# Another order for the prologue and for the bridge between the two halves of a fused Mamba-2 and ternary-expert layer

## The chip, the cores and the metric

The kernel runs on one core of one Trainium2 chip. The metric is the device time of one execution in microseconds (us), the median of several. Five engines have their own instruction streams: TensorE (PE; its weight loads are shown apart as PEld), VectorE (DVE), ScalarE (ACT), GpSimd (POOL) and SyncE (SP, which here only issues DMAs). They meet through semaphores.

## The reference, cut to what matters

```python
def reference(u, ...):                      # u: (2, 2048, 512) float32
    zxbcdt = einsum('bld,ed->ble', u, W_in)          # 2184 outputs: z, x, B, C, dt
    dt  = softplus(zxbcdt[..., -8:] + dt_bias)
    xBC = silu(conv1d_depthwise_4_taps(xBC) + conv_b)
    y   = ssd(x, dt, -exp(A_log), B, C, D)           # chunked state-space scan, 8 heads of 128
    yg  = y * silu(z)
    yn  = yg * rsqrt(mean(yg*yg) + 1e-5) * norm_w
    x1  = layernorm(u + yn @ W_out.T)
    # expert: ternary weights, scale = mean|W|, q = clip(round(W/scale), -1, 1) * scale
    h   = silu(x1 @ up_q.T) * (x1 @ gate_q.T)        # 2048 hidden
    return layernorm(x1 + h @ down_q.T)
```

## The kernel before, in words

Everything is float32, multiplied as pairs of reduced-precision parts: a tensor is split into a high part (suffix `hi` or `h`, made by a copy on ACT) and the rest (`lo` or `l`, a subtraction on DVE or POOL), and three products (or two, with the exact ternary weights) stand for one.

**First half.** The 4096 tokens are done in 16 groups (n = 0 to 15) of 256 tokens, each of two chunks (c = 2n, 2n+1) of 128 tokens. For each group PE runs nine steps `ip(n, k)` of the input projection: k = 0 is feature tile 16 (B and C), k = 1 to 4 are tiles 8 to 15 (x), k = 5 to 8 are tiles 0 to 7 (z). They go round three PSUM banks, so that step r = 9n + k waits until what step r - 3 left has been read, by the convolution taps (`f_taps`, on DVE) or by the gate's activation (`f_zs`, on ACT). Between them stand the small products: `DT`, `dtT` and `CUM` for the time steps, `G` for C times B, the transposes `TR`, and per chunk `Y` (the output of the scan), `ST` (its state), `SQ` (the mean square) and `OP` (the output projection). On the other engines, `f_xe` empties a bank into the convolution, `f_silc` is the SiLU behind it (it needs `f_edge` on POOL, which carries the edge between groups), `f_seg`, `f_E` and `f_M` build the decay matrix, `f_DI` (POOL) finishes it, `f_xTe` empties the transposes, `f_gate` multiplies Y by the gate, `f_r1` and `f_x1` are the first layer norm.

**Prologue.** Groups 0 and 1 run while the weights are still being split. `split_in(j)` splits tile j of W_in: first the high part on ACT, in `WHI_ORDER`, then the low part on DVE (tiles of `DVE_LO`) or on POOL (tiles of `POOL_LO`). PE waits on a count of these, so a tile is free only when all tiles ahead of it in its list are done. `split_out(k)` does the same for W_out, by `WOHI_ORDER` (ACT) and `WOLO_ORDER` (DVE). All this is written out call by call, one list for each engine. Groups 2 to 15 then follow in a loop, each with the same body.

**The bridge.** Behind group 15 (c = 30 and 31 are its chunks) PE finishes the last chunks, transposes the first 512 tokens of x1 (`T1`, from `load_x1(0)`) and starts the expert for them (token group g = 0): 16 tiles j, each with `expert(j, 0)` (up), `expert(j, 1)` (gate) and `down(j)`. Its weights are made ternary on the fly: `load_tern(j)` on SP, `ternary(j)` on DVE (three comparisons at L1038, three selections at L1042). `f_sil`, `f_h`, `f_hh`, `f_hl` make and split the hidden values, and `down(j)` waits for `f_hl(j)`. Into the last third of this stretch the preparation of the next 512 tokens is laid: the transposes `TX(1, i)`, and `f_xa`, `f_xb`, `f_xd`, `f_xh`, `f_xl`, `f_th`, `f_tl`. Their halves are used from `pair_a(0)` on.

**Second half.** Token groups 1 to 7 run as 56 steps Q, each a pair of expert tiles in a form with seven products instead of eight (`pair_a`, `pair_b`, `pair_b3`, `pair_c`, L421), with `down` (L494) between them. The sums of weights that it needs are made by POOL the first time (`f_S123`, `f_S4`, L1336 to L1345), stored, and read back afterwards.

All orders are fixed in the program text. An engine that waits holds up everything behind the waiting call in its own list.

## Time and profile before

| | |
|---|---|
| device time, three runs | 1492.88, 1498.31 (the median), 1498.94 us |
| the profiled execution's own time | 1492.88 us |
| its span, first to last instruction | 1491.1 us |
| PE busy | 1467.0 us (98% of the span) |
| DVE, ACT, POOL busy | 1109.8, 885.6, 428.9 us |
| granted TensorE clock, mean | 0.998 of full speed |
| DMA | 151.36 MB, 102 GB/s over the span |

The busy shares are for the whole span. The prologue is the stretch up to about 84 us, where the loop over the groups begins. The bridge begins at about 760 us and ends at 876.5 us, where `pair_a(0)` starts. PE's matmuls overlap, so a matmul of 0.4 us starts some 0.23 us behind the one before it.

### The profile page before, as it was taken

To read this page: it belongs to the slowest core of one execution; us is meant where nothing else is said; L and a number is where in the kernel's file an instruction comes from. 1 tells how busy PE (TensorE), PEld (TensorE's weight loads), DVE (VectorE), ACT (ScalarE), POOL (GpSimd) and SP (SyncE) were. 2 spreads that over 40 slices of the span, in tenths; PEclk is the share of its full clock that TensorE was granted. 3 is DMA by queue.
4 is the path that set the end of the run, shared out by engine and by line. 5 is a ranking of instruction groups with operands and counts; after the bars stand their busy time and mean duration, and the time that the engine had idled before them with its cause. 6 is when DMAs were issued, how large, how long until landed. Compare 5 with 4: busy or idle time off the path is not lost.

```text
span 1491.1 us, 27358 instructions
## 1 busy us (share of the span) xinstructions
PE 1467.0 (98%) x10356; PEld 1315.5 (88%) x10356; DVE 1109.8 (74%) x2376; ACT 885.6 (59%) x1688; POOL 428.9 (29%) x536
## 2 busy tenths in 40 slices
PE   8999999999999999999989999999999999999997
PEld 8888898888888898889877789899999998999996
DVE  7877887788877887789779967766656666665655
ACT  8777767766677767766762244545454454545442
POOL 4344454444434454445451116300000000000000
PEclk9999999999999999999999999999999999999999
DMA  7111222022211222122244404343343434334341
GB/s 263 65 49 66 93 72 93 27 88 85 80 50 65 93 72 77 38 93 72 79 163 167 151 29 152 104 156 100 107 149 106 149 107 149 102 112 142 98 135 64
DMA packets 64050, 151.36 MB, mean 102 GB/s; under 512 B 6960, under 2 KB 7472, under 8 KB 63920
## 3 DMA queue, kind: packets, MB, share of 16 engines
q1 hardware_dynamic: 63920, 149.62, 30.1%
q8 instruction: 82, 1.34, 0.4%
q14 instruction: 48, 0.39, 0.1%
HBM read 124.30 MB, written 25.30 MB: 100 GB/s over the span
## 4 chain that ended last, share of the span: by engine, by line
PE 88%; DMA 5%; DVE 4%; ACT 1%; issue 1%; SPq 0%; POOL 0%; POOLq 0%; DVEq 0%; ACTq 0%
PE ps L258 25%; PE ps L421 23%; PE ps L494 13%; PE ps L347 11%; PE ps L301 3%; PE ps L411 3%; DMA s_S<-wsum_scratch 2%; PE ps L309 2%; PE ps L318 2%; PE ps L288 2%; DMA out_dram<-s_x1n 1%; PE ps L388 1%; DVE s_ltm L1038 1%; PE ps L274 1%; PE ps L231 1%
## 5 line engine op out<-in xcount | busy, mean ns | idle before, releaser
L258 PE MATMUL ps<-s_uhi,s_whi 128*128 128x256 f32 x1088 | 313.6, 288 | 3.6 <-POOL s_wlo L1254 1.8
L258 PE MATMUL ps<-s_uhi,s_wlo 128*128 128x256 f32 x1088 | 306.2, 281 | 0.0
L258 PE MATMUL ps<-s_ulo,s_whi 128*128 128x256 f32 x1088 | 306.2, 281 | 0.0
L421 PE MATMUL ps<-s_xoh,s_S 128*128 128x256 f32 x896 | 222.9, 285 | 2.8 <-DMA s_S<-wsum_scratch 2.5
L421 PE MATMUL ps<-s_xol,s_S 128*128 128x256 f32 x896 | 220.5, 282 | 0.0
L258 PEld LDWEIGHTS ps<-s_uhi,s_whi 128*128 128x128 f32 x1088 | 204.9, 188 | 9.0 <-issue 5.9
L258 PEld LDWEIGHTS ps<-s_ulo,s_whi 128*128 128x128 f32 x1088 | 205.1, 189 | 0.0
L258 PEld LDWEIGHTS ps<-s_uhi,s_wlo 128*128 128x128 f32 x1088 | 204.8, 188 | 0.0
L494 PE MATMUL ps<-s_tern,s_hh 128*128 128x512 f32 x504 | 199.3, 395 | 0.0
L494 PE MATMUL ps<-s_tern,s_hl 128*128 128x512 f32 x504 | 198.7, 394 | 0.0
L421 PEld LDWEIGHTS ps<-s_xoh,s_S 128*128 128x128 f32 x896 | 169.2, 189 | 12.8 <-DMA s_S<-wsum_scratch 4.9
L421 PEld LDWEIGHTS ps<-s_xol,s_S 128*128 128x128 f32 x896 | 169.6, 189 | 3.9
L1321 POOL TENSOR_TENSOR s_lnb<-s_lnb,s_cst 128x1 f32<-128x1 f32 x32 | 19.0, 597 | 515.4 <-DVE s_lnb L1169 515.4
L421 PE MATMUL ps<-s_xol,s_tern 128*128 128x256 f32 x672 | 164.2, 281 | 0.0
L421 PE MATMUL ps<-s_xoh,s_tern 128*128 128x256 f32 x672 | 164.2, 281 | 0.0
L869 DVE SCALAR_TENSOR_TENSOR s_xact<-ps,s_pm,s_xact 128x256 f32<-128x256 f32 x384 | 154.4, 473 | 0.8 <-ACT s_xact L587 0.7
L421 PEld LDWEIGHTS ps<-s_xoh,s_tern 128*128 128x128 f32 x672 | 126.5, 188 | 2.4
L421 PEld LDWEIGHTS ps<-s_xol,s_tern 128*128 128x128 f32 x672 | 126.4, 188 | 2.5
L948 DVE SCALAR_TENSOR_TENSOR s_mm<-s_mm,s_dtv,s_gm 128x128 f32<-128x128 f32 x256 | 116.7, 527 | 9.3 <-ACT s_mm L634 9.3
L1283 POOL TENSOR_TENSOR s_mm<-s_mm,s_di 128x1024 f32<-128x1024 f32 x32 | 77.4, 2418 | 141.1 <-DVE s_mm L948 141.1
L494 PEld LDWEIGHTS ps<-s_tern,s_hh 128*128 128x128 f32 x504 | 95.0, 188 | 14.9
L494 PEld LDWEIGHTS ps<-s_tern,s_hl 128*128 128x128 f32 x504 | 95.4, 189 | 14.4
(182 smaller groups left out, 3105.6 us busy)
## 6 DMA issues: line engine op xcount, KB each, us to landing
s_S<-wsum_scratch SPq DMA_DIRECT2D x48, 512.0 KB, 3.7
s_S<-wsum_scratch SPq DMA_DIRECT2D x96, 256.0 KB, 3.3
s_bcx<-ct_scratch SPq DMA_DIRECT2D x32, 512.0 KB, 4.8
s_wst<-in_wffn SPq DMA_DIRECT2D x48, 256.0 KB, 2.8
s_wraw<-in_wffn SPq DMA_DIRECT2D x16, 768.0 KB, 10.3
s_uraw<-in_uT SPq DMA_DIRECT2D x16, 512.0 KB, 3.7
s_rr<-in_un SPq DMA_DIRECT2D x32, 256.0 KB, 4.6
x_scratch<-s_rr SPq DMA_DIRECT2D x32, 256.0 KB, 2.4
```

The costliest lines, as they stand in the source:

```text
L258: o = e.matmul(IPB[r % 3][:, 256 * i:256 * i + 256], wt[:, j, kk, :], u[:, kk, :], start=(m == 0), stop=(m == 11))
L288: o = e.transpose(B0[half][:, 128 * i:128 * i + 128], xact[:, 4 * half + i, 128 * (c % 2):128 * (c % 2) + 128], ident)
L301: o = e.matmul(B0[a][:, 128 * i:128 * i + 128], xT[:, c % 3, 4 * a + i, :], mm[:, c % 2, 4 * a + i, :], start=(i == 0), stop=fresh(c) and ...
L309: o = e.matmul(B0[a][:, 128 * i:128 * i + 128], st[r, i, :], cx[r, c % 2, i, :], start=False, stop=(i == 3), skip_group_check=True)
L318: o = e.matmul(B3[64 * a:64 * a + 64, :], btr[:, c % 4, :], xw[:, c % 2, 4 * a:4 * a + 4, :].rearrange("p h s -> p (h s)"), start=True, st ...
L347: o = e.matmul(B2[:], y[:, h, :], wt[:, h, :], start=(m == 0), stop=(m == 23))
L411: o = e.matmul(bank[:], tern[:, j, 512 * mi + 128 * k:512 * mi + 128 * k + 128], x[:, k, :], start=(m == 0), stop=(m == 7))
L421: o = e.matmul(bank[:, 256 * mi:256 * mi + 256], wt(mi, k), xo[g % 2][:, x, k, :], start=(first and mi == 0 and k == 0 and xo is xoh), sto ...
L494: o = e.matmul(DB[c][:], y[:, 128 * c:128 * c + 128], tern[:, j, 1024:1536], start=(j == 0 and lo == 0), stop=(j == 15 and lo == 1))
L869: o = e.scalar_tensor_tensor(dst, bank[:, 256 * i:256 * i + 256], convw[:, f, 3 - shift:4 - shift], dst, mult, add)
L948: o = e.scalar_tensor_tensor(mm[:, m2, h, :], mm[:, m2, h, :], dtv[:, n % 2, 8 * odd + h:8 * odd + h + 1], gm[:, c % 4, :], mult, mult)
L1283: e.tensor_tensor(mm[:, c % 2, :, :], mm[:, c % 2, :, :], di[:], add).then_inc(s_DI, 1)
```

## The change

Nothing is added or removed. The same calls, with the same bodies, are put into another order, in two places: the prologue up to the loop, and the bridge up to `pair_a(0)`. The loop bodies of groups 2 to 15 and of the 56 pair steps are as before. Among other things:

- the split of the W_in tiles is dealt out anew: DVE now does the low parts of 16, 8, 9, 10 and 11, POOL the other twelve, in another order; the high parts come in another order too
- on PE, `dtT(0)` goes behind `ip(0, 1)`, `CUM(0)` behind `ip(0, 3)`, `TR(0, 0)` behind `dtT(1)`, `G(1)` ahead of `Y(0)`, and `ip(1, 4)` between `Y(0)` and `ST(0)`
- on ACT, `f_seg(1)` now stands ahead of `f_uhi(1)`, `f_zs(0, 3)` and `f_E(1)` stand ahead of `f_xe(1, 0)`, and `f_silc(1, 0)` ahead of `f_xTe(1, 1)`
- on SP, `load_r0` for chunks 0 and 1 comes later (chunk 1 behind `store_ct(2)`), and in the bridge `load_x1(1)`, which waits for `OP(31)`, comes behind `load_tern(7)` instead of behind `load_tern(4)`
- in the bridge, `Y(30)` goes ahead of `ST(30)`, `T1(0)` between; `f_E(31)` and `f_M(31)` are earlier; the calls of `down` come at other places, and `down(10)` and `down(11)` now stand ahead of `expert(13, 0)`

```diff
@@ -179,11 +179,11 @@
...
-    DVE_LO = [9, 8, 11, 12, 5]
-    WHI_ORDER = [16, 8, 9, 10, 12, 13, 11, 15, 0, 6, 2, 3, 14, 7, 1, 4, 5]
-    POOL_LO = [16, 10, 13, 14, 15, 1, 0, 6, 2, 3, 4, 7]
-    WOHI_ORDER = [0, 2, 4, 6, 1, 3, 5, 7]
-    WOLO_ORDER = [2, 0, 4, 3, 6, 7, 1, 5]
+    DVE_LO = [16, 8, 9, 10, 11]
+    WHI_ORDER = [16, 8, 9, 10, 12, 11, 13, 14, 15, 1, 0, 2, 3, 4, 7, 6, 5]
+    POOL_LO = [12, 13, 14, 0, 15, 1, 2, 3, 7, 6, 5, 4]
+    WOHI_ORDER = [2, 0, 4, 6, 3, 1, 5, 7]
+    WOLO_ORDER = [0, 4, 3, 2, 1, 6, 5, 7]
@@ -507,9 +507,9 @@
...
-        warm(); ip(0, 0); DT(0); dtT(0); ip(0, 1); ip(0, 2); CUM(0); ip(0, 3); ip(0, 4); G(0); ip(0, 5); ip(0, 6)
-        TR(0, 0); DT(1); ip(0, 7); ip(0, 8); dtT(1); TR(0, 1); ip(1, 0); ip(1, 1); TR(1, 1); TR(1, 0); CUM(1)
-        ip(1, 2); ip(1, 3); ip(1, 4); Y(0); ST(0); G(1); ip(1, 5); Y(1); OP(0); SQ(0); ip(1, 6); ip(1, 7); ip(1, 8)
+        warm(); ip(0, 0); DT(0); ip(0, 1); dtT(0); ip(0, 2); ip(0, 3); CUM(0); ip(0, 4); G(0); ip(0, 5); ip(0, 6)
+        DT(1); ip(0, 7); ip(0, 8); dtT(1); TR(0, 0); TR(0, 1); ip(1, 0); ip(1, 1); TR(1, 1); CUM(1); TR(1, 0)
+        ip(1, 2); ip(1, 3); G(1); Y(0); ip(1, 4); ST(0); ip(1, 5); Y(1); OP(0); SQ(0); ip(1, 6); ip(1, 7); ip(1, 8)
@@ -518,13 +518,13 @@
...
         c = NCH - 2
-        OP(c - 1); T1(1); WT(); ST(c); Y(c); T1(0); Y(c + 1); SQ(c); T1(2); T1(3); OP(c); expert(0, 0); expert(0, 1)
+        OP(c - 1); T1(1); Y(c); T1(0); WT(); ST(c); Y(c + 1); T1(2); SQ(c); T1(3); OP(c); expert(0, 0); expert(0, 1)
...
-        expert(4, 0); expert(4, 1); down(0); down(1); expert(5, 0); down(2); expert(5, 1); expert(6, 0); expert(6, 1)
-        down(3); expert(7, 0); down(4); expert(7, 1); expert(8, 0); expert(8, 1); expert(9, 0); expert(9, 1); down(5)
-        TX(1, 0); expert(10, 0); down(6); expert(10, 1); expert(11, 0); expert(11, 1); down(7); expert(12, 0); down(8)
-        TX(1, 1); expert(12, 1); expert(13, 0); down(9); expert(13, 1); expert(14, 0); down(10); expert(14, 1)
-        expert(15, 0); expert(15, 1); down(11)
+        expert(4, 0); expert(4, 1); down(0); expert(5, 0); down(1); expert(5, 1); down(2); expert(6, 0); expert(6, 1)
+        down(3); expert(7, 0); expert(7, 1); expert(8, 0); down(4); expert(8, 1); expert(9, 0); expert(9, 1); TX(1, 0)
+        expert(10, 0); down(5); down(6); down(7); expert(10, 1); expert(11, 0); expert(11, 1); down(8); expert(12, 0)
+        TX(1, 1); down(9); expert(12, 1); down(10); down(11); expert(13, 0); expert(13, 1); expert(14, 0)
+        expert(14, 1); expert(15, 0); expert(15, 1)
@@ -767,16 +767,16 @@
...
-        f_uhi(0); split_in(16); split_in(8); split_in(9); expA(); split_in(10); f_xe(0, 0); split_in(12); split_in(13)
-        split_in(11); split_in(15); split_in(0); f_spexp(0); f_silc(0, 0); f_xe(0, 1); split_in(6); split_in(2)
-        split_in(3); split_in(14); split_in(7); f_xe(0, 2); split_in(1); split_in(4); f_silc(0, 1); f_xe(0, 3)
-        wabs(0); f_silc(0, 2); f_xe(0, 4); split_out(0); split_in(5); f_silc(0, 3); f_seg(0); split_out(2)
-        f_silc(0, 4); f_seg(1); f_zs(0, 0); f_zs(0, 1); split_out(4); f_E(0); f_uhi(1); f_spexp(1); f_xTe(0, 0)
-        f_zs(0, 2); f_xTe(0, 1); split_out(6); f_zs(0, 3); wabs(1); f_xe(1, 0); f_dec(0); f_xe(1, 1); f_xTe(1, 0)
-        split_out(1); f_E(1); split_out(3); split_out(5); f_xe(1, 2); f_xe(1, 3); f_dec(1); f_xTe(1, 1); f_silc(1, 0)
-        f_silc(1, 1); split_out(7); f_xe(1, 4); f_silc(1, 2); f_sq(0); f_ygh(0); wabs(2); wabs(3); f_seg(2)
-        f_silc(1, 3); f_zs(1, 0); f_sq(1); f_zs(1, 1); f_ygh(1); f_zs(1, 2); f_silc(1, 4); f_seg(3); f_xTe(2, 0)
-        f_xTe(2, 1)
+
+        f_uhi(0); split_in(16); split_in(8); expA(); f_xe(0, 0); split_in(9); split_in(10); split_in(12); split_in(11)
+        split_in(13); split_in(14); f_xe(0, 1); split_in(15); f_spexp(0); split_in(1); split_in(0); f_silc(0, 0)
+        split_in(2); split_in(3); f_xe(0, 2); split_in(4); split_in(7); f_xe(0, 3); f_silc(0, 1); f_silc(0, 2)
+        wabs(0); f_xe(0, 4); split_in(6); f_silc(0, 3); split_in(5); split_out(2); f_silc(0, 4); split_out(0)
+        f_seg(0); split_out(4); f_zs(0, 0); f_zs(0, 1); f_E(0); f_seg(1); f_uhi(1); split_out(6); f_spexp(1); wabs(1)
+        f_xTe(0, 0); f_zs(0, 2); f_zs(0, 3); split_out(3); f_xTe(0, 1); f_E(1); f_dec(0); f_xe(1, 0); f_xTe(1, 0)
+        split_out(1); f_xe(1, 1); split_out(5); f_xe(1, 2); f_silc(1, 0); f_xTe(1, 1); f_xe(1, 3); f_dec(1)
+        f_silc(1, 1); split_out(7); f_sq(0); f_ygh(0); f_xe(1, 4); wabs(2); f_silc(1, 2); wabs(3); f_seg(2); f_ygh(1)
+        f_sq(1); f_zs(1, 0); f_silc(1, 3); f_zs(1, 1); f_zs(1, 2); f_silc(1, 4); f_seg(3); f_xTe(2, 0); f_xTe(2, 1)
...
             c = 2 * n - 2
@@ -796,11 +796,11 @@
...
         c = NCH - 2
-        f_xTe(c + 1, 1); f_zs(NG - 1, 3); f_E(c + 1); f_xTe(c + 1, 0); f_x1h(0); f_x1h(1); f_ygh(c); f_sq(c); f_x1h(3)
-        f_x1h(2); f_sil(0); f_sil(1); f_ygh(c + 1); f_sq(c + 1); f_sil(2); f_hh(0); f_hh(1); f_hh(2); f_sil(3)
-        f_sil(4); f_hh(3); f_sil(5); f_hh(4); f_sil(6); f_hh(5); f_sil(7); f_sil(8); f_hh(6); f_hh(7); f_hh(8)
-        f_sil(9); f_sil(10); f_xa(1, 0); f_hh(9); f_xh(1, 0); f_sil(11); f_hh(10); f_sil(12); f_xa(1, 1); f_sil(13)
-        f_hh(11); f_hh(12); f_th(1, 0); f_sil(14); f_xh(1, 1); f_hh(13); f_th(1, 1); f_hh(14); f_sil(15); f_hh(15)
+        f_E(c + 1); f_xTe(c + 1, 1); f_xTe(c + 1, 0); f_zs(NG - 1, 3); f_x1h(0); f_sq(c); f_ygh(c); f_x1h(1); f_x1h(3)
+        f_x1h(2); f_ygh(c + 1); f_sil(0); f_sq(c + 1); f_sil(1); f_hh(0); f_sil(2); f_hh(1); f_sil(3); f_sil(4)
+        f_hh(2); f_hh(3); f_sil(5); f_hh(4); f_sil(6); f_hh(5); f_sil(7); f_hh(6); f_sil(8); f_hh(7); f_sil(9)
+        f_hh(8); f_xa(1, 0); f_sil(10); f_hh(9); f_hh(10); f_xh(1, 0); f_sil(11); f_sil(12); f_xa(1, 1); f_hh(11)
+        f_th(1, 0); f_xh(1, 1); f_th(1, 1); f_sil(13); f_hh(12); f_sil(14); f_hh(13); f_hh(14); f_sil(15); f_hh(15)
@@ -1172,13 +1172,13 @@
...
-        f_ulo(0); split_in(9); split_in(8); setup(); f_dte(0); f_taps(0, 0); f_dtr(0); split_in(11); split_in(12)
-        f_dA(0); f_taps(0, 1); f_cte(0); f_taps(0, 2); f_taps(0, 3); f_GM(0); f_dd(0); f_taps(0, 4); split_in(5)
-        skip_diag(); f_dte(1); split_out(2); f_dd(1); split_out(0); split_out(4); f_dtr(1); f_ulo(1); f_dA(1); f_M(0)
-        f_taps(1, 0); f_cte(1); f_wz(0); f_taps(1, 1); f_M(1); split_out(3); f_taps(1, 2); f_gate(0, 0); f_GM(1)
-        f_gate(0, 1); f_S(0); split_out(6); split_out(7); split_out(1); split_out(5); f_sqsum(0); f_taps(1, 3)
-        f_taps(1, 4); f_gate(1, 0); f_gate(1, 1); f_ms(0); f_wz(1); f_dd(2); f_r1(0); f_sqsum(1); f_x1(0); f_S(1)
-        f_dd(3)
+        f_ulo(0); split_in(16); split_in(8); setup(); f_dte(0); split_in(9); f_taps(0, 0); split_in(10); f_dtr(0)
+        split_in(11); f_dA(0); f_taps(0, 1); f_cte(0); f_taps(0, 2); f_taps(0, 3); f_taps(0, 4); f_GM(0); skip_diag()
+        f_dte(1); split_out(0); split_out(4); f_dd(0); f_dd(1); f_dtr(1); f_ulo(1); f_dA(1); f_M(0); split_out(3)
+        f_cte(1); f_taps(1, 0); f_taps(1, 1); f_wz(0); f_M(1); f_taps(1, 2); f_gate(0, 0); split_out(2); f_S(0)
+        split_out(1); f_gate(0, 1); split_out(6); split_out(5); f_GM(1); split_out(7); f_sqsum(0); f_taps(1, 3)
+        f_taps(1, 4); f_gate(1, 0); f_wz(1); f_ms(0); f_gate(1, 1); f_sqsum(1); f_r1(0); f_dd(2); f_dd(3); f_S(1)
+        f_x1(0)
...
             c = 2 * n - 2
@@ -1193,14 +1193,14 @@
...
         c = NCH - 2
-        f_ms(c - 1); f_r1(c - 1); f_M(c + 1); f_gate(c, 0); f_gate(c, 1); f_x1l(1); f_S(c); f_sqsum(c); scales()
-        f_ms(c); f_x1l(0); f_x1l(2); ternary(0); f_x1l(3); ternary(1); f_gate(c + 1, 0); f_gate(c + 1, 1); f_h(0)
-        ternary(2); f_sqsum(c + 1); f_r1(c); ternary(3); f_h(1); ternary(4); f_x1(c - 1); f_hl(0); f_ms(c + 1)
-        f_hl(1); f_h(2); f_r1(c + 1); f_hl(2); f_h(3); ternary(5); f_h(4); ternary(6); f_hl(3); ternary(7); f_h(5)
-        f_hl(4); f_x1(c); f_hl(5); ternary(8); f_h(6); ternary(9); f_h(7); f_hl(6); f_h(8); ternary(10); f_x1(c + 1)
-        f_hl(7); f_hl(8); f_xb(1, 0); f_h(9); ternary(11); f_h(10); f_hl(9); ternary(12); f_xd(1, 0); f_h(11)
-        f_hl(10); ternary(13); f_xb(1, 1); ternary(14); f_h(12); f_xd(1, 1); ternary(15); f_hl(11); f_hl(12); f_h(13)
-        f_xl(1, 0); f_xl(1, 1); f_tl(1, 0); f_tl(1, 1); f_h(14); f_hl(13); f_hl(14); f_h(15); f_hl(15)
+        f_ms(c - 1); f_M(c + 1); f_r1(c - 1); f_gate(c, 0); f_gate(c, 1); scales(); f_S(c); f_x1l(1); f_sqsum(c)
+        f_x1l(0); f_ms(c); ternary(0); f_x1l(2); f_x1l(3); ternary(1); f_gate(c + 1, 0); f_gate(c + 1, 1); ternary(2)
+        f_sqsum(c + 1); f_h(0); f_x1(c - 1); f_hl(0); f_r1(c); f_h(1); ternary(3); f_h(2); ternary(4); f_ms(c + 1)
+        ternary(5); f_r1(c + 1); f_hl(1); f_hl(2); f_h(3); f_h(4); f_x1(c); f_hl(3); ternary(6); f_h(5); ternary(7)
+        f_hl(4); f_h(6); f_hl(5); ternary(8); f_h(7); f_hl(6); ternary(9); f_h(8); ternary(10); f_hl(7); f_h(9)
+        f_hl(8); ternary(11); f_xb(1, 0); f_hl(9); f_h(10); f_xd(1, 0); f_xl(1, 0); ternary(12); f_h(11); f_x1(c + 1); f_xb(1, 1)
+        ternary(13); f_hl(10); f_xd(1, 1); f_xl(1, 1); f_hl(11); f_h(12); f_tl(1, 0); ternary(14); f_tl(1, 1); f_hl(12); f_h(13)
+        ternary(15); f_hl(13); f_h(14); f_hl(14); f_h(15); f_hl(15)
@@ -1351,10 +1351,10 @@
...
-        split_in(16); split_in(10); split_in(13); split_in(14); split_in(15); split_in(1); split_in(0); split_in(6)
-        f_Cexp(0); split_in(2); f_edge(0, 0); split_in(3); f_edge(0, 1); f_edge(0, 2); split_in(4); f_edge(0, 3)
-        f_edge(0, 4); split_in(7); f_DI(0); f_xw(0); f_edge(1, 0); f_DI(1); f_Cexp(1); f_edge(1, 1); f_edge(1, 2)
-        f_ygl(0); f_edge(1, 3); f_Sd(1); f_rs(0); f_edge(1, 4); f_rs1(0); f_xw(1); f_ygl(1)
+        f_edge(0, 0); split_in(12); split_in(13); split_in(14); split_in(0); split_in(15); split_in(1); split_in(2)
+        split_in(3); split_in(7); split_in(6); f_edge(0, 1); f_edge(0, 2); split_in(5); f_edge(0, 3); split_in(4)
+        f_DI(0); f_edge(0, 4); f_Cexp(0); f_edge(1, 0); f_xw(0); f_edge(1, 1); f_DI(1); f_Cexp(1); f_edge(1, 2)
+        f_ygl(0); f_Sd(1); f_xw(1); f_rs(0); f_edge(1, 3); f_edge(1, 4); f_ygl(1); f_rs1(0)
...
             c = 2 * n - 2
@@ -1367,8 +1367,8 @@
...
         c = NCH - 2
-        f_rs(c - 1); f_DI(c); f_DI(c + 1); f_Sd(c); f_Cexp(c + 1); f_rs(c); f_ygl(c); f_ygl(c + 1); f_rs1(c - 1)
-        f_rs(c + 1); f_rs1(c); f_rs1(c + 1); f_S123(0); f_S4(0)
+        f_DI(c); f_rs(c - 1); f_Cexp(c + 1); f_Sd(c); f_DI(c + 1); f_ygl(c); f_ygl(c + 1); f_rs1(c - 1); f_rs(c)
+        f_rs(c + 1); f_rs1(c); f_S123(0); f_S4(0); f_rs1(c + 1)
@@ -1483,8 +1483,8 @@
...
-        load_r0(0); store_ct(1); load_u(2); load_wst(2); load_wst(3); load_bc(2); load_bc(3); load_r0(1); store_x1(0)
-        load_wst(4); store_ct(2); load_wst(5); load_wst(6)
+        store_ct(1); load_u(2); load_wst(2); load_bc(2); load_bc(3); load_wst(3); load_wst(4); load_r0(0); store_ct(2)
+        load_wst(5); load_r0(1); load_wst(6); store_x1(0)
...
             c = 2 * n - 2
@@ -1496,10 +1496,10 @@
...
         c = NCH - 2
-        load_tern(0); load_x1(0); load_r0(c); load_tern(1); load_tern(2); load_tern(3); load_tern(4); load_x1(1)
-        load_r0(c + 1); load_tern(5); load_tern(6); load_tern(7); load_tern(8); load_tern(9); load_tern(10)
-        load_tern(11); store_x1(c - 1); load_tern(12); store_x1(c); load_tern(13); load_tern(14); store_x1(c + 1)
-        load_tern(15)
+        load_tern(0); load_x1(0); load_tern(1); load_tern(2); load_tern(3); load_r0(c); load_tern(4); load_tern(5)
+        load_r0(c + 1); load_tern(6); load_tern(7); load_x1(1); load_tern(8); load_tern(9); load_tern(10)
+        load_tern(11); store_x1(c - 1); load_tern(12); load_tern(13); load_tern(14); load_tern(15); store_x1(c)
+        store_x1(c + 1)
```

## Rows read from the trace of the kernel before

**Rows 1.** Busy time by engine in four stretches (with instructions), granted clock, DMA share and rate.

```profile
0.00:41.00 41.00, 34.78 (x266) 32.26 (x267) 28.32 (x79) 34.31 (x68) 18.12 (x34) 1.00 0.67 239
41.00:84.00 43.00, 42.18 (x331) 38.01 (x331) 35.76 (x86) 34.21 (x69) 19.56 (x25) 1.00 0.20 68
...
755.00:786.00 31.00, 26.70 (x180) 21.32 (x177) 21.42 (x47) 19.77 (x33) 16.02 (x10) 1.00 0.53 195
786.00:877.00 91.00, 90.85 (x399) 72.79 (x400) 86.91 (x150) 25.94 (x40) 11.34 (x9) 1.00 0.35 130
```

**Rows 2.** Waits of PE in the whole span: who waited for whom, total, times, longest.

```profile
PE ps L258 <- POOL s_wlo L1254: 1.8, 1, 1.8
PE ps L258 <- DVE s_ulo L854: 1.8, 1, 1.8
PE ps L369 <- DMA s_x1n<-x_scratch: 1.6, 1, 1.6
PE ps L336 <- DVE s_wsc L1026: 1.3, 1, 1.3
...
PE ps L301 <- DVE s_ygr L975: 0.9, 1, 0.9
PE ps L288 <- ACT s_xact L605: 0.9, 1, 0.9
PE ps L347 <- DVE s_wolo L831: 0.8, 1, 0.8
PE ps L238 <- DVE s_dts L881: 0.7, 1, 0.7
```

**Rows 3.** Timeline of ACT: start, duration, line, operation, out<-in, count [idle before <-releaser].

```profile
38.34 1.06 ACT L564 ACTIVATE s_uhi<-s_uraw 128x1024 fp32r<-128x1024 f32 x1 [0.98 <-PE ps L258]
...
43.97 0.57 ACT L587 ACTIVATE s_bcacc<-ps,s_pm 128x256 f32<-128x256 f32 x1
```

**Rows 4.** Groups of ACT, 13 to 76 us: count, busy us, mean ns, idle before.

```profile
L598 ACT ACT_TABLE_LOAD x2 | 2.6, 1283 | 0.0
...
L634 ACT ACTIVATE s_mm<-s_mm 128x1024 f32<-128x1024 f32 x2 | 2.1, 1059 | 0.0
```

**Rows 5.** Timeline of the DMA queue's issues on SP, store_ct(2).

```profile
102.32 0.32 SPq L1393 DMA_DIRECT2D ct_scratch<-s_cts  x1
```

**Rows 6.** Landing time of load_r0(1), the one load of rr issued between 60 and 72 us.

```profile
DMA to landing us min/median/max: 5.6/5.6/5.6
```

**Rows 7.** Timeline of DVE: f_M(0), f_r1(1), f_M(3), and the comparisons of ternary(8).

```profile
43.58 2.19 DVE L948 SCALAR_TENSOR_TENSOR s_mm<-s_mm,s_dtv,s_gm 128x128 f32<-128x128 f32 x8
...
105.93 0.74 DVE L1007 SCALAR_TENSOR_TENSOR s_rr<-ps,s_lnb,s_rr 128x512 f32<-128x512 f32 x1
...
107.72 4.32 DVE L948 SCALAR_TENSOR_TENSOR s_mm<-s_mm,s_dtv,s_gm 128x128 f32<-128x128 f32 x8
...
825.45 4.41 DVE L1038 TENSOR_SCALAR s_ltm<-s_wraw,s_wsc 128x512 bf16<-128x512 f32 x3
```

**Rows 8.** Timeline of POOL: f_DI(30), and the first and last of f_S123(0) and f_S4(0).

```profile
765.61 2.37 POOL L1283 TENSOR_TENSOR s_mm<-s_mm,s_di 128x1024 f32<-128x1024 f32 x1
...
824.90 1.80 POOL L1336 TENSOR_TENSOR s_S<-s_tern 128x512 fp32r<-128x512 f32 x1 [12.53 <-issue]
...
829.54 1.48 POOL L1345 TENSOR_TENSOR s_S<-s_tern,s_S 128x512 fp32r<-128x512 f32 x1
```

**Rows 9.** Groups of DVE, 833 to 877 us.

```profile
L1042 DVE SCALAR_TENSOR_TENSOR s_tern<-s_wraw,s_wsc,s_ltm 128x512 fp32r<-128x512 f32 x21 | 14.5, 748 | 0.0
L1038 DVE TENSOR_SCALAR s_ltm<-s_wraw,s_wsc 128x512 bf16<-128x512 f32 x21 | 8.9, 482 | 0.0
```

**Rows 10.** Timeline of PE: matmuls that begin expert(0, 0), expert(13, 1), down(10).

```profile
786.02 0.50 PE L411 MATMUL ps<-s_x1h,s_tern 128*128 128x512 f32 x1 [0.39 <-DVE s_x1l L1048]
...
863.46 0.40 PE L411 MATMUL ps<-s_x1h,s_tern 128*128 128x512 f32 x1
...
867.19 0.40 PE L494 MATMUL ps<-s_tern,s_hh 128*128 128x512 f32 x1
```

## Prediction

> **What bounds the kernel now.** I read four views, in this order. First the windows over the two stretches that the change touches [rows 1]: the second column is PE's busy time, and the reader is to see that PE is full nearly everywhere, at a granted clock of 1.00, so that the only time to be had without taking matmuls away is PE's idle time. It is 6.2 us up to 41 us, 0.8 us from 41 to 84 us, 4.3 us from 755 to 786 us and 0.2 us from 786 to 877 us. Then PE's waits [rows 2]: each of the idle spells has a name. In the prologue these are the first low part (1.8), `f_dte(0)` ahead of `dtT(0)` (0.7), `f_silc(0, 4)` ahead of `TR(0, 0)` (0.9), `f_ulo(1)` ahead of `ip(1, 0)` (1.8) and the last `split_out` ahead of `OP(0)` (0.8). In the bridge they are the load of x1 ahead of `T1(1)` (1.6), `f_gate(30)` ahead of `Y(31)` (0.9), `scales` ahead of `SQ(30)` (1.3) and `f_x1l(3)` ahead of `expert(0, 0)` (0.4, [rows 10]). The sum is 10.2 us, 0.7% of the time, and it is the most that an order can give back here. Third the timelines of ACT, DVE and POOL, to see who is late, and last the DMA queue, for what stands behind a waiting `store_ct`.
>
> Since PE is full behind both stretches, whatever is won or lost at `DT(2)` (83.3 us) or at `pair_a(0)` (876.5 us) is carried to the end unchanged. So the forecast is two differences. I followed every list of the changed order call by call with the durations of the same calls in this trace; I give the steps that decide.
>
> **Prologue, up to `ip(1, 0)`: a gain of 1.2 us.** The low part of tile 16 goes to DVE, which is free only behind `f_ulo(0)` but needs less time than POOL: ready about 0.5 us sooner, so PE starts 0.5 us sooner. With `ip(0, 1)` ahead of `dtT(0)` the wait of 0.7 us is covered. `ip(0, 2)` then waits some 0.4 us for tile 10, the fourth on DVE's list, and `ip(0, 4)` 0.3 us for the taps of step 1. `TR(0, 0)` no longer stands in front, which saves its 0.9 us, but `ip(0, 7)` begins with tile 4, the last on POOL's list, and waits 0.4 us. `ip(0, 8)` ends at about 35.9 instead of 38.2 us. What is late next is ACT: `f_seg(1)` now stands ahead of `f_uhi(1)`, which began 0.1 us behind `ip(0, 8)` before [rows 3] and now begins 1.2 us behind it. So `f_ulo(1)` ends at 39.5, and `ip(1, 0)` starts at 39.5 instead of 40.7 us: of 2.3 us won, 1.2 are left, and PE's wait there is 2.3 us.
>
> **Prologue, from `ip(1, 0)` on: all of that is given back, and 1.0 us more.** ACT is busy 68.5 of the first 84 us [rows 1], and its list decides. `f_zs(0, 2)` ends at 42.1 us by my count, since the copy for `f_xTe(0, 0)`, a `split_out`, a `wabs` and a table load (1283 ns, [rows 4]) stand ahead of it; `ip(1, 1)` wants that bank at 41.2 us: 1.0 us of waiting. Then `f_E(1)` (a table load, 1.06 us for the decay matrix [rows 4], 1.3 us for the other exponentials) stands ahead of `f_xe(1, 0)`, which moves from 44.0 [rows 3] to 47.3 us. Behind it come the taps, the edge on POOL, and on ACT five more calls and a table load before the three activations of `f_silc(1, 0)`; they end at about 54.0 us. `G(1)` is now ahead of `Y(0)`, at 52.4 us on PE's list: 1.6 us of waiting, where before it stood behind `ST(0)` and waited for nothing. The other moves on PE are covered: `ST(0)`'s `f_xw(0)` is done at 54.5, `Y(1)`'s gates at 62.5 against 63.4 us, the last `split_out` at 65.1 against `OP(0)` at 66.3 us, so the wait of 0.8 us there is gone. Behind `OP(0)` PE's list is unbroken up to `DT(2)`, which waits 0.3 us for `f_ms(1)`, now behind `f_x1(0)` on DVE. `DT(2)` comes at 84.3 instead of 83.3 us: **+1.0 us**. ACT runs two more table loads than before, both ahead of `f_silc(1, 1)`, where nobody waits.
>
> **`load_r0(1)`.** It now stands behind `store_ct(2)`, issued at 102.3 us [rows 5], or 103.3 with the shift, and behind `load_wst(5)`: issue at 104.2. It needed 5.6 us to land [rows 6], which makes 109.8 us. `f_r1(1)` wants it at 105.9 + 1.0 = 106.9 us [rows 7]. DVE stands still for up to 2.9 us, and `f_M(3)` is queued behind it, then `f_DI(3)` on POOL and `Y(3)` on PE. `f_M(3)` took 4.3 us because POOL ran beside it; the same call took 2.2 us with POOL idle [rows 7], and later it would meet less of POOL. `f_DI(3)` was done 1.2 us ahead of `Y(3)`. Bounds: nothing, if what `f_M(3)` saves makes up for it, or 2.9 - 1.2 = 1.7 us. I take **+0.2 us**, near the lower end, since the two savings together (1.2 and up to 2.1) exceed the delay.
>
> **Bridge, up to `expert(0, 0)`: -0.4 us.** `T1(1)` stays where it was, at 768.0 us: `load_x1(0)` is issued at the same place, with as much traffic behind it. `f_E(31)` without its two table switches is done 3.8 us sooner, and `Y(30)` can follow `T1(1)` at once. But `f_M(31)` now runs beside POOL's `f_xw(30)`, `f_DI(30)` and `f_Cexp(31)` and ends only at about 769.8, so that `f_gate(30)` is no sooner than `Y(30)`, and `f_DI(31)` (2.4 us, [rows 8]) is queued behind `f_Sd(30)`, which waits for `Y(30)`: 771.75 + 1.0 + 2.4 = 775.2 us, where `Y(31)` started at 774.3. That is 0.9 us later. It is made up at once: the wait of 1.3 us for `scales` becomes one of about 0.3, now for `f_sqsum(30)` and `f_ms(30)`; `OP(30)` starts at 779.8 us as before, and `f_x1l(3)` is ready at 783.7, so its 0.4 us fall away.
>
> **Bridge, `expert(0, 0)` to `pair_a(0)`: +1.0 us.** Two experts take 3.73 us [rows 10], one matmul 0.233 us. 376 matmuls (32 experts, 12 downs, `OP(31)`) and 1.7 us for transposes and `SQ(31)` make 89.4 us; before it took 90.5, so about 1.0 us of short waits is hidden in it, all in places that the new order leaves (**-1.0**). Against that stands the end of the stretch. One `ternary` costs DVE 3 x 0.48 + 3 x 0.75 us less overlap [rows 9], 3.2 us. `f_h(10)` can run when `expert(11, 0)` is through, at 848.4 us in the new order. Behind it on DVE stand `f_xd(1, 0)`, `f_xl(1, 0)`, `ternary(12)`, `f_h(11)`, `f_x1(31)`, `f_xb(1, 1)` (not before `TX(1, 1)`, 856.7), `ternary(13)`, and only then `f_hl(10)`: done at 861.2. `down(10)` wants it at 860.3: 0.9 us. `f_hl(11)` follows behind `f_xd(1, 1)` and `f_xl(1, 1)` at 864.0, and `down(11)`, now directly behind `down(10)`, wants it at 863.1: 1.0 us. Before, two experts lay between [rows 10]. That is **+1.9 us**; the later experts find their `ternary` in time by 0.3 us or more.
>
> One thing more. `store_x1(29)`, for which POOL's `f_S123(0)` waits, is issued behind fewer loads and lands at about 816 instead of 825 us. The four operations last from 824.90 to 831.02 us [rows 8], and beside them the comparisons of one `ternary` took 4.41 us [rows 7] instead of 3 x 0.48 [rows 9]; with its selections, 4.2 us more. Now that falls on `ternary(7)`. `expert(7, 0)` is 0.9 us away, and `ternary(8)` comes 0.7 us late for `expert(8, 0)`. Bounds: 0 (if it falls on DVE's idle time ahead of `f_h(5)`) and 0.7; I take **+0.4 us**. So the stretch is -1.0 + 1.9 + 0.4 = +1.3, and the bridge +0.9 with the -0.4 ahead of it. In the section "Who interferes with whom" of the page "SBUF — State Buffer" the Trainium skill says that of a DVE and a GpSimd instruction that need the shared port the later one blocks fully. By that the whole 6.1 us of POOL would be lost, not 4.2, and the sum would be higher by up to 1.9 us; the row of `f_M(3)`, slowed by 2.1 us beside 2.6 us of POOL, lies between.
>
> **Sum.** 1.0 + 0.2 - 0.4 + 1.3 = +2.1 us, against the profiled execution's 1492.88 us (span 1491.1 and 1.8 us around it): 1495.0 us. The runs lie on two levels, 1492.9 and 1498.3 to 1498.9; the profile is of the lower one, the median 5.4 us above it. Against the median: 1498.3 + 2.1 = 1500.4 us.
>
> **Rivals.**
> - *The waits go and nothing takes their place.* If `f_silc(1, 0)` is ready at 52.4 us instead of 54.0, `f_zs(0, 2)` at 41.2 instead of 42.1 and `f_hl(10)` by 860.3, the prologue ends 1.6 us ahead and the bridge 1.4 us ahead: 1495 us, still no change that counts. All 10.2 us would give 1488.1. Against it: three lists would each have to be over 1 us faster than their own durations. It decides (over 0.5%) only from 7.5 us on, three quarters of all idle time.
> - *The load of x1 comes late.* `load_tern(1)` to `(3)` stand directly behind `load_x1(0)`. If the DMA engines mix them, 2.4 MB at 195 GB/s [rows 1] put `T1(1)` up to 12 us later, and everything is behind it: 1512 us. Against it: before, four loads of weights and one of u stood behind it too, and PE waited 1.6 us.
> - *DVE loses to `f_S123(0)` and `f_S4(0)` the whole time that POOL needs for them*, 831.02 - 824.90 = 6.1 us [rows 8] and not 4.2: then `expert(8, 0)` waits 0.7 + 1.9 = 2.6 us instead of 0.4, and the time is 1502.6 us. Against it: beside the same four operations DVE did lose only 4.2 us here.
> - *The order changes nothing that counts*: DVE and ACT find slack that I did not see, between -1 and +1 us: 1498.3 us.
>
> **How the numbers follow.** Forecast (+1 to +4 us) 0.45; nothing (-1 to +1) 0.20; a gain of 1 to 7.5 us 0.15; DVE loses all of POOL's time, or several short waits more (+4 to +7.5) 0.08; over 7.5 us slower 0.08 (the late load 0.05, another list that stalls 0.03); over 7.5 us faster 0.04. A change of 0.5% (7.5 us) is about what a measurement of this kernel can tell from none; its own runs lie 6 us apart. Faster 0.04, same 0.88, slower 0.08. The range has to take in both levels of the runs: below, the lower level with nothing changed or a little won, 1492; above, the upper level with +7.5, 1506.
>
> **What would show it.** In the changed kernel's profile: PE's first `ip` at 7.4 us; a wait of PE for `f_ulo(1)` of about 2.3 us; waits of L258 for `f_zs` (1.0) and of L274 for `f_silc(1, 0)` (1.6), both new; `DT(2)` (L231) at 84.3; DVE waiting at L1007 for the load of rr near 107 us; the wait for `f_x1l` gone; waits of L494 for `f_hl` (0.9 and 1.0) near 860 us; `pair_a(0)` at 878 to 879 us. The prediction is wrong if `DT(2)` comes ahead of 83 or behind 87 us, if `T1(1)` moves by more than 1 us, or if PE gets idle time behind 880 us that it did not have.

## Result, and the profile after

The changed kernel took 1506.8 us (median of five runs, 1504.8 to 1509.2), the kernel before 1495.8 on the same chip (1492.9 to 1498.9). The ratio is 1.0072, with a 95% interval of 1.0050 to 1.0093: slower by 0.7%, where the forecast was +2.1 us. The profiled execution took 1502.94 us (span 1501.1, 1.8 around it), 10.1 more than that of before.

First the windows of the changed kernel over the stretches of [rows 1]: PE busy in the second column, granted clock third from the end.

```profile
0.00:41.00 41.00, 30.12 (x210) 27.50 (x211) 32.53 (x68) 25.89 (x52) 17.67 (x32) 0.88 0.66 233
41.00:84.00 43.00, 39.29 (x303) 35.91 (x302) 33.60 (x86) 35.94 (x69) 15.26 (x18) 1.00 0.19 62
```

PE has lost 4.7 us of work in the first 41 us, and the mean clock there is 0.88. Who held it up is in PE's waits, the answer to [rows 2]:

```profile
PE ps L266 <- DVE s_sc L918: 6.7, 2, 6.4
PE ps L258 <- DVE s_wlo L827: 2.2, 2, 1.7
PE ps L494 <- DVE s_hl L1100: 1.8, 2, 1.0
PE ps L301 <- POOL s_mm L1283: 1.8, 1, 1.8
...
PE ps L258 <- DVE s_ulo L854: 1.5, 1, 1.5
PE ps L274 <- ACT s_cd L602: 1.4, 1, 1.4
PE ps L258 <- DVE s_xact L869: 1.2, 1, 1.2
...
PE ps L258 <- ACT s_zs L571: 0.8, 1, 0.8
PE ps L336 <- DVE s_sqs L993: 0.6, 1, 0.6
```

The waits that I had named are there, near their sizes (f_hl 1.8, G(1) 1.4, f_zs 0.8). The largest isn't one of them: `CUM(0)` (L266) waits 6.4 us for the last operation of `f_dA(0)` (L918). DVE's timeline shows why that is late:

```profile
15.04 1.25 DVE L897 TENSOR_SCALAR s_sc<-s_sc 128x16 f32<-128x16 f32 x1
16.33 0.25 DVE L899 RECIPROCAL s_sc<-s_sc 128x16 f32<-128x16 f32 x1
16.62 0.92 DVE L901 TENSOR_TENSOR s_sc<-s_sc 128x16 f32<-128x16 f32 x1
17.57 1.22 DVE L903 TENSOR_TENSOR s_sc<-s_sc 128x16 f32<-128x16 f32 x1
18.82 1.20 DVE L905 TENSOR_SCALAR s_sc<-s_sc 128x16 f32<-128x16 f32 x1
20.06 5.27 DVE L908 SCALAR_TENSOR_TENSOR s_sc<-s_sc 128x16 f32<-128x16 f32 x6
25.36 0.17 DVE L910 SCALAR_TENSOR_TENSOR s_sc<-s_sc 128x16 f32<-128x16 f32 x1
```

and POOL's, what lies beside it:

```profile
13.18 11.70 POOL L1254 TENSOR_TENSOR s_wlo<-s_wlr,s_whi 128x512 fp32r<-128x512 f32 x9
```

`f_dA` is fifteen operations of 128x16 (L897 to L918), nearly all of which need the result of the one before; the expectation of `p7_pool_short_reads` says sixteen. Each needs 0.17 us by itself (L910), the reciprocal 0.25. In the new order POOL's splits of W_in run back to back from 13.2 to 24.9 us (11.70 / 9 = 1.3 us each), and as long as they do, a link of the chain lasts about 1.2 us, one POOL instruction; the reciprocal alone does not. Eight of the fifteen were held so, the last ones ran when POOL had stopped. The chain took 10.9 us instead of 3.0. In the kernel before the same chain (13.9 to 16.9 us) lay in a pause of POOL, 12.6 to 19.0 us.

The wait has a second effect. These windows of the changed kernel show the clock around it:

```profile
15.00:20.00 5.00, 4.54 (x36) 4.34 (x36) 4.86 (x6) 4.92 (x10) 5.00 (x5) 1.00 0.82 306
20.00:22.00 2.00, 0.00 (x0) 0.00 (x0) 1.93 (x3) 2.00 (x6) 2.00 (x2) 1.00 0.00 0
22.00:24.00 2.00, 0.00 (x0) 0.00 (x0) 1.93 (x3) 0.43 (x1) 2.00 (x3) 0.56 0.00 0
24.00:32.00 8.00, 4.68 (x20) 4.17 (x21) 7.83 (x24) 1.57 (x3) 0.88 (x1) 0.50 0.23 61
32.00:33.00 1.00, 1.00 (x9) 1.00 (x8) 1.00 (x4) 0.30 (x2) 0.00 (x0) 0.75 0.92 348
33.00:40.00 7.00, 7.00 (x62) 6.66 (x64) 5.92 (x15) 6.26 (x15) 4.57 (x9) 1.00 0.96 330
```

PE is idle from 19.7 us; the granted clock goes from 1.00 (2.4 GHz) to 0.50 (1.2 GHz) and comes back at 32 to 33 us, when PE has worked again for six. `ip(0, 4)` falls into that: 4.9 us instead of 3.1, and the four products of `CUM(0)` 1.1 instead of 0.7.

Last, PE's timeline where the parts of the prediction end: `ip(1, 0)`, `DT(2)`, `expert(0, 0)`, `down(10)` and `down(11)`, and `pair_a(0)` (before: 40.71, 83.28, 786.02 and 876.51 us).

```profile
49.07 0.39 PE L258 MATMUL ps<-s_uhi,s_whi 128*128 128x256 f32 x1 [1.51 <-DVE s_ulo L854]
...
93.89 0.64 PE L231 MATMUL ps<-s_uraw,s_wdr 128*32 128x256 f32 x8 [0.17 <-DVE s_lnb L1000]
...
795.86 0.40 PE L411 MATMUL ps<-s_x1h,s_tern 128*128 128x512 f32 x1
...
871.54 0.51 PE L494 MATMUL ps<-s_tern,s_hh 128*128 128x512 f32 x1 [0.84 <-DVE s_hl L1100]
...
874.67 0.50 PE L494 MATMUL ps<-s_tern,s_hh 128*128 128x512 f32 x1 [1.00 <-DVE s_hl L1100]
...
887.78 0.29 PE L421 MATMUL ps<-s_xoh,s_tern 128*128 128x256 f32 x1
```

| part of the sum | forecast | measured |
|---|---|---|
| prologue up to `ip(1, 0)` | -1.2 | +8.4 (49.07 - 40.71) |
| from there to `DT(2)` | +2.2 | +2.2 (44.82 for 42.57) |
| `load_r0(1)`, groups 2 to 15 | +0.2 | 0 |
| bridge up to `expert(0, 0)` | -0.4 | -0.8 |
| `expert(0, 0)` to `pair_a(0)` | +1.3 | +1.4 (91.92 for 90.49) |
| behind `pair_a(0)` | 0 | -1.3 |
| sum | +2.1 | +10.0 (spans) |

The -1.3 behind `pair_a(0)`, where both kernels are the same, is no effect of the order: over the profiles of all versions that stretch took between 612.9 and 617.8 us (before 614.6, after 613.3).

### The profile page after: what moved, and what is told of

It reads as the page before. It is cut to its first block, busy times and chain, and to the rows that moved or that the text cites. A ratio compares the mean times of both kernels' runs of the same rounds, so it can differ in the third digit from the quotient of the medians.

```text
span 1501.1 us, 27357 instructions
## 1 busy us (share of the span) xinstructions
PE 1469.8 (98%) x10356; PEld 1317.8 (88%) x10356; DVE 1121.8 (75%) x2376; ACT 885.5 (59%) x1688; POOL 427.9 (29%) x536
## 4 chain that ended last, share of the span: by engine, by line
PE 88%; DVE 4%; DMA 3%; ACT 2%; issue 1%; SPq 0%; POOL 0%; POOLq 0%; DVEq 0%; ACTq 0%
PE ps L258 24%; PE ps L421 23%; PE ps L494 14%; PE ps L347 12%; PE ps L411 4%; PE ps L301 3%; DMA s_S<-wsum_scratch 2%; PE ps L309 2%; PE ps L318 2%; PE ps L288 2%; DMA out_dram<-s_x1n 1%; PE ps L388 1%; PE ps L274 1%; PE ps L231 1%; DVE s_sc L908 0%
## 5 line engine op out<-in xcount | busy, mean ns | idle before, releaser
L494 PE MATMUL ps<-s_tern,s_hh 128*128 128x512 f32 x504 | 199.5, 396 | 1.8 <-DVE s_hl L1100 1.8
L494 PE MATMUL ps<-s_tern,s_hl 128*128 128x512 f32 x504 | 198.7, 394 | 0.0
L948 DVE SCALAR_TENSOR_TENSOR s_mm<-s_mm,s_dtv,s_gm 128x128 f32<-128x128 f32 x256 | 123.3, 553 | 9.4 <-ACT s_mm L634 9.4
L494 PEld LDWEIGHTS ps<-s_tern,s_hh 128*128 128x128 f32 x504 | 95.0, 188 | 17.4 <-DVE s_hl L1100 2.7
L494 PEld LDWEIGHTS ps<-s_tern,s_hl 128*128 128x128 f32 x504 | 95.4, 189 | 14.3
## 6 DMA issues: line engine op xcount, KB each, us to landing
s_wraw<-in_wffn SPq DMA_DIRECT2D x16, 768.0 KB, 10.9
```

The costliest lines, as they stand in the source:

```text
L494: o = e.matmul(DB[c][:], y[:, 128 * c:128 * c + 128], tern[:, j, 1024:1536], start=(j == 0 and lo == 0), stop=(j == 15 and lo == 1))
L948: o = e.scalar_tensor_tensor(mm[:, m2, h, :], mm[:, m2, h, :], dtv[:, n % 2, 8 * odd + h:8 * odd + h + 1], gm[:, c % 4, :], mult, mult)
```

## The experiments

**The two places apart.** `s1_prologue` has the new lists and loads of the prologue alone, `s2_bridge` those of the bridge alone.

> The new lists of all engines up to group 1 and SP's moved loads there, with the old bridge and experts. Theory (the whole loss lies in the prologue, 10.6 us at DT(2), and nothing of it is made up in groups 2 to 15): DT(2) at 93.9, the last OP of the groups 10.6 later than in the kernel before, pair_a(0) 10.6 later as well (887.1), time 1505 to 1507. Rival (the bridge or the hand-over to it shares in the loss or hides some of it): pair_a(0) more than 1 us away from 887.1.

> The old prologue with the new bridge and experts. Theory: the two halves of the change don't touch one another, so DT(2) stays at 83.3, expert(0, 0) starts 0.8 us earlier than before (785.2), the experts up to pair_a(0) take 1.4 us more because of the two waits of down(10) and down(11), pair_a(0) at 877.1; time within 0.1% of the kernel before. Rival (what the kernel after gained behind pair_a(0), 1.3 us, belongs to the bridge too): faster by 1 us or so, still within 0.5%.

`s1_prologue`: 1504.7 us, ratio 1.0072 (1.0058 to 1.0086), the whole loss. `DT(2)` came at 95.5 and `pair_a(0)` at 890.5 us, 14.0 later than before and not 10.6. Of the 3.4 us more, 1.6 were there at `DT(2)` already: in this execution the first products came 0.21 us apart instead of 0.12 (though the profile's clock reads 1.00 there), and `ip(0, 2)` waited 2.9 us instead of 0.5 for a split that DVE made beside POOL. The rest came in the bridge, where the clock was 0.94 in the mean from 755 to 786 us. By its rival's own mark, `pair_a(0)` more than 1 us away from 887.1, this expectation missed; the median, 1504.7 against 1505 to 1507, was close.

`s2_bridge`: 1495.9 us, ratio 1.0007 (0.9997 to 1.0016), no change; its two waits for f_hl were there (1.8 us). `expert(0, 0)` stood 704.3 us behind `DT(2)`, in the kernel before 702.7 and in the kernel after 702.0; here too the clock was 0.94 in the bridge, so that this run can't confirm the 0.8 us gained there. The profiles of the runs below do: where the clock was 1.00, that distance was 701.9 to 702.4 us with the new bridge (`p1`, `p4`, `p5`, `p6`, `p9`) and 702.6 to 703.0 with the old one (`p2`, `p3`, `p7`, `p8`). From there to `pair_a(0)` it took 92.6 us in `s2_bridge`, 91.9 to 93.0 in the other profiles with the new lists and 90.5 to 91.6 with the old ones. So the new bridge wins some tenths of a us up to 1, and the new order of the experts loses 1.4 to 2.5 against the kernel before.

**`s3_late_downs`: the last two `down` put apart again**, on top of `s2_bridge`:

```diff
-        expert(12, 1); down(10); down(11); expert(13, 0); expert(13, 1); expert(14, 0)
+        expert(12, 1); expert(13, 0); down(10); expert(13, 1); expert(14, 0); down(11)
```

> As s2_bridge, but down(10) stands behind expert(13, 0) and down(11) behind expert(14, 0). Theory (the two waits of 0.8 and 1.0 us there are for halves of h that VectorE makes later, and nothing else is lost): both waits gone, pair_a(0) at 875.3 to 875.8, 1.0 us or so ahead of the kernel before, time about 0.1% below it, which the times alone can't tell from no change. Rival (the waits only move on to the next product that needs VectorE, expert or down): waits of the same sum elsewhere between 865 and 877, pair_a(0) at 877.

The rival held. PE's timeline has no wait of L494 any more, and this in its place:

```profile
872.07 0.50 PE L411 MATMUL ps<-s_x1h,s_tern 128*128 128x512 f32 x1 [1.94 <-DVE s_tern L1042]
```

1.9 us for a `ternary`, where it had been 1.8 us for `f_hl`. `expert(0, 0)` to `pair_a(0)` took 91.8 us (before 90.5), the ratio was 1.0016 (1.0007 to 1.0026). Both are waits for DVE, of one size; between these two orders PE's list decided only which call met it.

**`p1_pool_held`: POOL kept still during `f_dA(0)`.** The kernel after, with one wait in POOL's list:

```diff
-        f_edge(0, 0); split_in(12); split_in(13); split_in(14); split_in(0); split_in(15); ...
+        f_edge(0, 0); split_in(12); split_in(13)
+        w.wait_ge(s_dA, 1)
+        split_in(14); split_in(0); split_in(15); ...
```

> The changed kernel, with one wait more: POOL does the low parts of tiles 12 and 13 and then waits for f_dA(0) before it goes on with tile 14. Nothing is left out. Port theory (f_dA(0) took 10.9 us instead of 3.0 because each of its short DVE instructions waited for the POOL instruction then running): f_dA(0) lasts about 4 us (one or two of its instructions still meet tiles 12 and 13), CUM(0) waits under 1 us instead of 6.4, the clock stays at 1.00, DT(2) starts at 84.5 to 86.5 instead of 93.9 us, and the time falls by 7 to 9 us. Rival (the chain is slow for another reason, such as the landing weights or its new place behind a split_in on DVE): f_dA(0) stays at 10 us or more, and since POOL's later tiles come later still, the time rises by some us.

1498.8 us, ratio 1.0028 (1.0015 to 1.0042): of 0.72% of loss 0.44 are gone, though POOL's splits came later. DVE's timeline of this kernel, with the two links that still met `split_in(12)` and `(13)` (POOL, 14.14 to 16.66 us) first:

```profile
14.61 0.86 DVE L889 TENSOR_SCALAR s_sc<-s_sc 128x16 f32<-128x16 f32 x1
15.50 1.19 DVE L891 SCALAR_TENSOR_TENSOR s_sc<-s_sc 128x16 f32<-128x16 f32 x1
...
17.22 0.16 DVE L897 TENSOR_SCALAR s_sc<-s_sc 128x16 f32<-128x16 f32 x1
...
18.33 1.23 DVE L908 SCALAR_TENSOR_TENSOR s_sc<-s_sc 128x16 f32<-128x16 f32 x6
```

`f_dA(0)` is back at 3.05 us and `CUM(0)` waits for nothing. `DT(2)` came at 87.4 us: 6.5 better than after, 0.9 beyond what I expected. PE's first products ran at half clock in this execution (0.50 from 8 to 11 us), and `dtT(0)` started at 13.9 us instead of 12.5.

**`p2_pool_reads`, `p7_pool_short_reads`: the same injury done to the kernel before.** POOL gets extra subtractions behind its `split_in(13)`, results unused: five of 128x512, or twenty of 128x128.

```diff
         split_in(16); split_in(10); split_in(13)
+        for i in range(5):                               # p7: range(20), 128 columns
+            ...
+            e.tensor_tensor(dst, hi[0], hi[1], sub).then_inc(s_cst, 1)
         split_in(14); split_in(15); ...
```

> The kernel before, with five extra POOL subtractions of 128x512 (read two tiles in SBUF, write a tile that nobody reads) behind its third split_in, where POOL stood idle from 12.6 to 19.0 us. The output is unchanged. Port theory: f_dA(0), now at 13.9 us, meets them and loses about 1.0 us in each instruction that starts while one of them runs: it takes 7 to 9 us instead of 3.1, CUM(0) waits 3 to 5 us, and TensorE's granted clock may fall. Rival (POOL's work has nothing to do with it): f_dA(0) stays at 3.1 us, and the prologue ends where it did, DT(2) at 83.3 us, or at most 1 us later.

> The kernel before with 20 more subtractions on GpSimd of 128x128, where p2_pool_reads had five of 128x512, all reading and writing SBUF in the same stretch. Theory (each short VectorE instruction waits out the one GpSimd instruction that is running): the sixteen short operations of f_dA(0) take the length of a GpSimd instruction each (0.3 to 0.4 us, estimated as a quarter of 1.28), f_dA(0) 5 to 6 us as far as it lies beside them, against 10.3 in p2_pool_reads. Rival (VectorE gets a fixed small share while GpSimd works, or is shut out until GpSimd pauses): short operations of 1.2 us or more, as before.

`p2_pool_reads`: `f_dA(0)` 10.3 us and 5.6 late, `CUM(0)` waits 9.2, `DT(2)` at 98.4, 1507.9 us in one run. First DVE, then POOL:

```profile
19.50 1.26 DVE L897 TENSOR_SCALAR s_sc<-s_sc 128x16 f32<-128x16 f32 x1
...
21.07 0.17 DVE L901 TENSOR_TENSOR s_sc<-s_sc 128x16 f32<-128x16 f32 x1
...
21.70 4.21 DVE L908 SCALAR_TENSOR_TENSOR s_sc<-s_sc 128x16 f32<-128x16 f32 x6
```

```profile
18.99 1.74 POOL L1360 TENSOR_TENSOR s_gap<-s_whi 128x512 f32<-128x512 f32 x1
22.15 7.38 POOL L1254 TENSOR_TENSOR s_wlo<-s_wlr,s_whi 128x512 fp32r<-128x512 f32 x6 [1.43 <-ACT s_whi L549]
```

The extra subtractions held what stands ahead of the chain on DVE, two short operations and two splits. Of the chain's own links one met the last of them (L897) and six met POOL's own splits from 22.15 us on; between the two, with POOL idle, the links took 0.17 us. So the kernel before, its order untouched, becomes as slow as the changed one when POOL is busy there.

`p7_pool_short_reads` tells the length from the mere presence; again DVE, then POOL:

```profile
16.47 0.38 DVE L905 TENSOR_SCALAR s_sc<-s_sc 128x16 f32<-128x16 f32 x1
16.89 2.45 DVE L908 SCALAR_TENSOR_TENSOR s_sc<-s_sc 128x16 f32<-128x16 f32 x6
19.37 0.38 DVE L910 SCALAR_TENSOR_TENSOR s_sc<-s_sc 128x16 f32<-128x16 f32 x1
```

```profile
16.79 0.46 POOL L1360 TENSOR_TENSOR s_gap<-s_whi 128x128 f32<-128x128 f32 x1
17.20 0.45 POOL L1360 TENSOR_TENSOR s_xw<-s_whi 128x128 f32<-128x128 f32 x1
```

A new POOL instruction every 0.41 us, a new link every 0.41 us: the chain (15.15 to 20.99 us) took 5.8 us (`DT(2)` at 90.2, 1498.9 us in one run). POOL worked back to back beside the slow links in both runs, so it is the length of its instruction that a link waits out, not a share of the time.

**`p3_pool_writes`, `p8_memset_in_dA`: POOL only writes.** Fourteen memsets (they fill a tensor with zeros) of 128x512 in the same place; in `p8` POOL first waits for what `f_dA(0)` waits for, so that they lie beside the chain.

```diff
+        w.wait_ge(s_spexp, 1)                            # p8 only
+        for i in range(14):
+            ...
+            e.memset(dst, 0.0).then_inc(s_cst, 1)
```

> As the run with five extra subtractions, but POOL runs 14 extra memsets of 128x512 there, which only write. If it is POOL's reading that blocks DVE, f_dA(0) takes 3.1 to 3.5 us and DT(2) comes at 83.3 us or so. If any POOL instruction blocks DVE, each of its some 17 instructions loses up to one memset (about 0.4 us), and f_dA(0) takes 7 to 9 us.

> The kernel before with 14 more memsets of 128x512 on GpSimd, that start together with f_dA(0) (in p3_pool_writes they ended before it). Theory (a stream of GpSimd writes without pause shuts VectorE's short operation out until it ends, whichever operation it is): the first of f_dA(0) beside them lasts nearly the whole 6.6 us and the rest 0.17 each, f_dA(0) 9.5 us in all. Rival (only the one-source operation of p3_pool_writes is shut out that way, and operations with two sources wait 0.5 us each, one memset): a long first operation, a tensor_scalar, if it meets them, but several of 0.3 to 0.6 us among the others. Second rival (writes of GpSimd don't touch operations with two sources): those stay at 0.17 while the memsets run.

In `p3` the memsets ran from 12.52 to 19.12 us, and one DVE operation of 128x16 lasted nearly as long:

```profile
12.29 6.86 DVE L889 TENSOR_SCALAR s_sc<-s_sc 128x16 f32<-128x16 f32 x1
19.19 0.17 DVE L891 SCALAR_TENSOR_TENSOR s_sc<-s_sc 128x16 f32<-128x16 f32 x1
```

`f_dA(0)` came behind them and took 3.05 us, so `p3` could not tell what memsets do to it; that is why `p8` was run. `ip(0, 2)` waited 4.5 us for the split behind the long operation, and `DT(2)` was at 90.4 (1498.6 us in one run).

In `p8` they lay from 13.85 to 20.54 us, over the whole chain:

```profile
14.38 0.48 DVE L897 TENSOR_SCALAR s_sc<-s_sc 128x16 f32<-128x16 f32 x1
...
15.40 0.17 DVE L903 TENSOR_TENSOR s_sc<-s_sc 128x16 f32<-128x16 f32 x1
15.61 0.22 DVE L905 TENSOR_SCALAR s_sc<-s_sc 128x16 f32<-128x16 f32 x1
15.86 1.22 DVE L908 SCALAR_TENSOR_TENSOR s_sc<-s_sc 128x16 f32<-128x16 f32 x6
17.12 0.18 DVE L910 SCALAR_TENSOR_TENSOR s_sc<-s_sc 128x16 f32<-128x16 f32 x1
17.21 0.52 DVE L911 TENSOR_SCALAR s_sc<-s_sc 128x16 f32<-128x16 f32 x1
```

The second rival held for operations with two tensors as sources: 0.17 to 0.18 us each in the middle of the memsets, where subtractions on POOL had cost them 1.2. The three `tensor_scalar` lasted 0.48, 0.22 and 0.52 us, at most one memset (0.52 to 0.55 us). Why that of `p3`, which began while POOL's last subtraction still ran, found no gap in fourteen of them stays open. `DT(2)` of `p8` was at 86.4, in one run of 1497.2 us.

**`p4_keep_clock`, `p5_keep_longer`: the half clock by itself.** The kernel after, with products that nobody reads between `ip(0, 3)` and `CUM(0)`; 14 in `p4`, 28 in `p5`. The profile records each of these float32 products as two matmuls, 28 and 56.

```diff
+        def keep():
+            for i in range(14):                          # p5: range(28)
+                e.matmul(B3[:, 0:128], xT[:, 0, 0, :], xT[:, 0, 0, :], start=True, stop=True)
...
-        ... ip(0, 2); ip(0, 3); CUM(0); ...
+        ... ip(0, 2); ip(0, 3); keep(); CUM(0); ...
```

> The changed kernel, with 14 products of zeros (128x128) on PE between ip(0, 3) and CUM(0), into a bank that is free there; they take about 6 us, which PE otherwise waits. The output is unchanged. Clock theory: the granted clock stays at 1.00 up to 41 us, ip(0, 4) takes 3.1 instead of 4.9 us, and DT(2) comes 1.5 to 2.5 us sooner than in the changed kernel (93.9), with f_dA(0) as long as there (10.9 us). Rival (the slower matmuls do not matter, since ip(0, 4) is followed by a wait for ACT or DVE anyway): ip(0, 4) is faster and DT(2) stays within 0.5 us.

> The kernel after with 56 products that nobody reads between ip(0, 3) and CUM(0), so that TensorE is busy through the 6.4 us in which it waited for f_dA(0). Theory (the half clock after the wait is a part of the loss of its own): granted clock 1.00 up to 41 us, ip(0, 4) 3.1 us and not 4.9, DT(2) 1.5 to 2.2 us earlier than in the kernel after (91.7 to 92.4). Rival (VectorE, late by 7.8 us, sets the pace to f_ulo(1), whatever the clock): the clock as above, but DT(2) at 93.9 again, and waits of TensorE for VectorE in place of the slow products.

`p4` missed its aim: the 28 matmuls took 3.3 us and not the expected 6, PE stood idle for another 3.3, the clock was 0.52 from 26 to 33 us, `DT(2)` at 94.0 and the time 1504.1 us in one run. In `p5` the fill was long enough; its windows:

```profile
20.00:60.00 40.00, 35.33 (x293) 33.27 (x292) 31.79 (x90) 31.45 (x64) 13.15 (x20) 1.00 0.32 111
63.00:67.00 4.00, 4.00 (x25) 3.93 (x25) 4.00 (x14) 3.90 (x8) 2.76 (x4) 0.65 0.00 0
```

`ip(0, 4)` took 3.1 us, and `ip(1, 0)` started at 48.11 instead of 49.07: 1.0 us is what the half clock costs there. The other half of it went into longer waits, for the taps (1.6 for 1.2) and for `f_ulo(1)` (2.1 for 1.5). `DT(2)` was at 94.5 all the same, since the clock fell between 63 and 67 us, behind no wait over 1.5 us (from `G(1)` to `DT(2)` it took 32.0 us, in the kernel after 30.4). The ratio was 1.0088 (1.0075 to 1.0101), no better than that of the kernel after.

**`p6_g1_late`, `p9_xte_first`: the loss behind `ip(1, 0)`.** On top of `p1_pool_held`, `G(1)` back behind `ST(0)`; in `p9` also ACT's `f_xTe(1, 1)` back ahead of `f_silc(1, 0)`:

```diff
-        ip(1, 2); ip(1, 3); G(1); Y(0); ip(1, 4); ST(0); ...        # PE
+        ip(1, 2); ip(1, 3); Y(0); ip(1, 4); ST(0); G(1); ...
-        ... f_xe(1, 2); f_silc(1, 0); f_xTe(1, 1); f_xe(1, 3); ...  # ACT, p9 only
+        ... f_xe(1, 2); f_xTe(1, 1); f_silc(1, 0); f_xe(1, 3); ...
```

> As p1_pool_held, and G(1) of TensorE stands behind ST(0) again. Theory (the wait of G(1) for ScalarE's decay is a real cost of its new place): no wait of G(1), and the stretch from the start of DT(1) to the start of DT(2), 54.9 us in p1_pool_held, is 53.5; time 1.4 us below p1_pool_held, ratio to before 1.002. Rival (the wait covers one that comes behind it): the wait turns up again at Y(1), ST(0) or the output projection, and the stretch stays at 54.9.

> As p6_g1_late, and on ScalarE f_xTe(1, 1) stands ahead of f_silc(1, 0) again. In p6_g1_late Y(0), which wants the transposes of chunk 1 too, waited 2.15 us for f_xTe(1, 1), directly behind f_silc(1, 0). Theory (what the prologue loses from ip(1, 0) on comes from these four calls of ScalarE standing ahead of that copy, a table load of 1.28 us among them): Y(0) waits for nothing, G(1) has what it needs when ST(0) is through, and the stretch from DT(1) to DT(2) is 53.3 us at the full clock (57.1 in p6_g1_late, less 1.7 for its stretch at half clock, less 2.15); time some 2 us below p6_g1_late. Rival (the next wait stands right behind: the gates or the last split_out on VectorE): a wait of 1 us or more at Y(1), ST(0) or L347 between 56 and 72 us, and the stretch at 54.5 or above.

In `p6` the rival held in substance: G(1)'s wait of 1.4 us went and one of 2.1 came, though at `Y(0)`, which the rival hadn't named.

```profile
57.58 0.68 PE L301 MATMUL ps<-s_mm,s_xT 128*128 128x128 f32 x4 [2.15 <-ACT s_xT L616]
```

`Y(0)` wants the transposes of chunk 1 as well, and their copy stood behind `f_silc(1, 0)` with its table load. In the kernel after, that copy ended at 64.0 and `Y(0)` started at 64.2 us: the wait of `G(1)` had only covered that of `Y(0)`. The stretch from `DT(1)` grew to 57.1 us, with a spell at half clock from 59 to 62 us in it. In `p9` neither waits, and from `ip(1, 0)` to `DT(2)` it took 43.7 us, against 44.9 in `p1` and 42.6 before. The stretch from `DT(1)` was 55.2, not 53.3: `ip(0, 7)` waited 2.5 us for POOL (1.1 in `p6`), which the held splits make late, and 0.4 us came up at `Y(1)`. The times don't tell the two apart: `p6` 1.0044 (1.0029 to 1.0058), `p9` 1.0040 (1.0027 to 1.0054), `p1` 1.0028.

No version ran faster than the kernel before.

## Why the prediction was wrong, step by step

**"Prologue, up to `ip(1, 0)`: a gain of 1.2 us" is the step that failed**; it measured +8.4. Its first sentences held: PE started at 7.37 us, the wait of `dtT(0)` was gone, `ip(0, 2)` waited 0.5. What failed is what all steps rest on, "the durations of the same calls in this trace": I took `f_dA(0)` at the 3.0 us of the trace, as work that costs PE nothing. In the new order it lies beside POOL's splits and took 10.9. Of the loss, 6.4 us is `CUM(0)`'s wait and 1.2 that of the taps (0.3 forecast), which are queued behind `f_dA(0)` on DVE; 2.2 us went to products at half clock, of which `p5` shows 1.0 to be on the path. `p1` and `p2` show the cause from both sides. Whether the 1.2 us would have come without it no run shows: in `p1` and `p9` the held splits make others late. One term of the step rested on a wrong reading of the lists: `f_seg(1)` stood ahead of `f_uhi(1)` before too, only further ahead. `f_uhi(1)` began 0.2 us behind `ip(0, 8)` and not 1.2, and PE's wait for `f_ulo(1)` was 1.5 us, not 2.3.

The rows to see it by were there. [Rows 7] and [rows 8] have three comparisons that took 4.4 us beside the first three of four POOL instructions, of 1.4 to 1.8 us: one each. I used that pair for the bridge as a price per microsecond of POOL (4.2 of 6.1), where the number of dependent DVE instructions was the measure, and did not ask which other DVE calls the new order puts beside POOL. For links of 0.17 us that is a factor of seven, for a split of 128x512 (0.68 us; 1.82 beside POOL in `s1_prologue`) less than three.

**"From `ip(1, 0)` on": +2.2 forecast, +2.2 measured**, with the waits in their places: f_zs 0.8 (I said 1.0), G(1) 1.4 (1.6), `DT(2)` 0.2 (0.3), none at `OP(0)`. That the sums meet is in part luck: with the 0.8 us saved at `OP(0)` the measured waits make +1.6, and the other 0.7 us is PE busy longer with the same calls (42.45 us for 41.75), which I hadn't forecast. And the step blamed G(1)'s new place, where `p6` shows that the wait only moves when G(1) goes back: ACT's order makes it, through `Y(0)`. `p9` gave 1.1 of the 2.2 back.

**`load_r0(1)`**: it was issued at 113.8 and landed in 2.8 us, not 5.6; `f_r1(1)` found it there (116.7). The lower bound, 0.

**Bridge**: `T1(1)` waited 0.4 us where I had left 1.6; x1 came 1.2 us sooner against `OP(29)`, so the rival of the late load fell. `Y(31)` waited 1.8 us for `f_DI(31)`, as the step has it. In sum -0.8 against -0.4, and the later profiles bear out a gain of some tenths up to 1 us.

**Experts**: waits of 0.84 and 1.00 us where 0.9 and 1.0 were forecast. Beside `f_S123(0)` the comparisons of a `ternary` did take 4.20 us, but no PE wait followed in this profile. In those of `s2`, `p1` and `p9` one did, 0.4, 0.8 and 0.8 us at 833 us, between and just above the bounds of 0 and 0.7: the +0.4 was a fair middle. `s3` adds that putting the two `down` later does not take their waits away. The step also set the row of `f_M(3)` between 4.2 of 6.1 us and the whole. By the trace POOL was busy for 3.2 us beside it and not 2.6, so that its 2.1 us are the same two thirds, and it spoke for nothing higher.

In "Who interferes with whom" of "SBUF — State Buffer" the Trainium skill has the later of two instructions blocked fully; by whole instructions of POOL the chain agrees (1.2 us a link, 0.41 with short ones). The same section has an operation with two SBUF inputs meet a GpSimd instruction that reads SBUF and not one that only writes it, and names `tensor_scalar` among the operations that can take the shared ports for themselves: `p8` agrees with both (0.17 us, and up to 0.52), while the 6.86 us of `p3` go beyond one instruction. I had weighed the rule for the bridge alone; laid beside `f_dA(0)` it speaks against this change.

**The base**: the forecast stood on a median of 1498.3 from three runs; five gave 1495.8. That hid 2.5 us of the error.

## What to carry to other kernels

- Before a list is moved, look for chains of short dependent operations on DVE and ask what POOL does beside them. Their cost there is the number of links that run while POOL works, times the length of one POOL instruction. Here keeping POOL quiet for that moment brought 6.5 us back, more than any short wait the new order removed.
- When all calls keep their bodies, their durations still don't stay: take them from rows with the same neighbour, or bound them by the slowest row of the same shape.
- A wait named in PE's list can cover another one behind it. Ask of each, before it is priced or cured, what the next call in the list waits for.

## What the runs showed of the hardware that I had not expected

- A DVE operation of 128x16 between SBUF tensors waits out one POOL subtraction (1.2 us beside 1.28, 0.4 beside 0.45). The reciprocal did not (0.25 us in every run).
- Memsets on POOL leave DVE's two-source operations at 0.17 us and can hold a `tensor_scalar`: by up to 0.35 us in `p8` and by 6.7 us in `p3`.
- Of the thirteen profiles of changed kernels all but that of `p9` show, in the first 96 us, a spell of about 3 us or more at half clock (1.2 GHz): behind a wait of PE of 2.7 us or more (after, `p2`, `p3`, `p4`, `p7`, `s1`, `s2`), or behind none over 2 us, as at 8 to 11 us in `p1`, 44 to 48 in `s3`, 63 to 67 in `p5`. The profile of the kernel before shows none there. One costs 1.0 us (after against `p5`) to 1.6 us (the spell of `p5`), as much as most steps of this prediction, and what sets off those of the second kind stays open.
